# ScalarE fetches two function tables at other places: the root's in a distance attention, the sigmoid's in a quantized gated layer

## The reference, cut to what matters

```python
p = softmax(where(mask, scores, -1e32)) * mask
cum, tot = cumsum(p), sum(p)
dist = sqrt(clip((tot - cum) * abs(i - j), 0))
effect = clip(exp(dist * -softplus(gammas) * exp(sigmoid(pdiff))), 1e-5, 1e5)
scores = softmax(where(mask, scores * effect, -1e32))      # row 0 set to 0
out = scores @ v
```

```python
def act_qdq(x):
    scale = maximum(max(abs(x)) / 32767, 1e-12)
    return clip(round(x / scale), -32768, 32767) * scale
x = act_qdq(x)
up, gate = act_qdq(x @ w_up.T), act_qdq(x @ w_gate.T)
sig = clip(round(sigmoid(gate) * 65536), 0, 65535) / 65536
out = act_qdq(act_qdq(gate * sig) * up) @ w_down.T
```

## Time and profile before

| | |
|---|---|
| median of 3 runs | 1441.05 us (1440.38 to 1443.08) |
| the profiled execution | 1447.14 us |
| its span | 1445.4 us |
| PE, PEld busy | 943.6 us (65%), 610.1 us (42%) |
| DVE busy | 1015.2 us (70%) |
| ACT busy | 627.9 us (43%) |
| POOL busy | 123.2 us (9%) |

### The profile page before, as it was taken

How to read it: one execution, slowest core, us unless ns; L and a number is a source line. 1 busy time by engine, 2 the same in 40 slices (tenths; PEclk the granted TensorE clock), 3 DMA queues, 4 the chain that set the end, 5 groups by cost and what they waited for, 6 DMA issues and landing times. The chain is left out here.

```text
span 1445.4 us, 18406 instructions
## 1 busy us (share of the span) xinstructions
PE 943.6 (65%) x6190; PEld 610.1 (42%) x6190; DVE 1015.2 (70%) x2541; ACT 627.9 (43%) x1329; POOL 123.2 (9%) x261
## 2 busy tenths in 40 slices
PE   4864757555884204455978636999778526967977
PEld 2532333333553103345945313666445223534644
DVE  4868989835554899874448574999578596957833
ACT  3646666622432404443126425655046302634632
POOL 0120000000000000000120120000011021120100
PEclk9975555557986557667989857999679757988968
DMA  5000000001334001112000000000000000000000
GB/s 190 2 1 0 1 1 1 1 1 44 91 90 150 1 0 61 47 44 59 1 1 2 1 1 0 1 1 1 0 1 1 1 0 1 2 1 1 2 1 15
DMA packets 25997, 29.51 MB, mean 20 GB/s; under 512 B 689, under 2 KB 22577, under 8 KB 24882
## 3 DMA queue, kind: packets, MB, share of 16 engines
q1 hardware_dynamic: 25906, 28.35, 6.2%
HBM read 18.91 MB, written 9.44 MB: 20 GB/s over the span
## 5 line engine op out<-in xcount | busy, mean ns | idle before, releaser
L1750 DVE TENSOR_TENSOR_SCAN l2a_hs<-l2a_decay,l2a_b_ps 128x512 f32<-128x512 f32 x64 | 78.0, 1221 | 14.3 <-ACT l2a_decay L1680 6.1
L1605 PEld LDWEIGHTS l2a_b_ps<-l2a_diag,l2a_uT 128*128 128x128 f32 x512 | 64.0, 191 | 39.3 <-issue 38.0
L1605 PE MATMUL l2a_b_ps<-l2a_diag,l2a_uT 128*128 128x128 f32 x512 | 69.9, 280 | 2.0 <-DVE l2a_hs L1750 1.7
L2170 PE MATMUL l1w_mem_ps<-l1w_rows,l1w_post 128*128 128x64 f32 x16 | 4.6, 381 | 96.9 <-DVE l1w_rows L2313 96.9
L1613 PE MATMUL l2a_acc_ps<-l2a_hc,pack 128*128 128x512 f32 x128 | 65.5, 595 | 1.0 <-DVE l2a_hc L1761 1.0
L2286 DVE MATCH_REPLACE8 l1w_minus<-l1w_low,l1w_minus 128x129 f32<-128x129 f32 (+39 forms) x264 | 64.9, 283 | 0.0
L2280 DVE MAX8 l1w_low<-l1w_minus 128x8 f32<-128x129 f32 (+37 forms) x332 | 60.1, 278 | 0.8 <-DVE l1w_minus L2266 0.5
L2198 ACT ACTIVATE l1w_score<-l1w_mix_ps 128x264 f32<-128x264 f32 (+7 forms) x29 | 12.0, 451 | 111.7 <-DVE l1w_rows L2313 92.5
L2160 PE MATMUL l1w_mix_ps<-l1w_rows,l1w_pre 128*128 128x264 f32 (+7 forms) x58 | 30.9, 707 | 45.4 <-DMA l1w_rows<-scores_dram 37.7
L1680 ACT ACTIVATE l2a_decay<-l2a_dt,pack 128x1016 f32<-128x1016 f32 x32 | 36.4, 1141 | 45.4 <-DVE l2a_hs L1750 45.4
L917 ACT ACTIVATE l0x_prob<-l0x_dist,l0x_last_mx 128x128 f32<-128x128 f32 x128 | 38.3, 387 | 21.5 <-DVE l0x_last_mx L1039 21.5
(11 more groups left out here) (586 smaller groups left out, 2720.1 us busy)
## 6 DMA issues: line engine op xcount, KB each, us to landing
scores_dram<-l1p_dots SPq DMA_DIRECT2D x8, 1056.0 KB, 6.8
l1w_rows<-scores_dram SPq DMA_DIRECT2D x8, 1056.0 KB, 5.1
pack<-in_pack SPq DMA_DIRECT2D x1, 697.5 KB, 9.5
pack<-in_pack SPq DMA_DIRECT2D x2, 321.5 KB, 6.6
pack<-in_pack SPq DMA_DIRECT2D x1, 612.0 KB, 11.5
pack<-in_pack SPq DMA_DIRECT2D x1, 576.0 KB, 10.4
pack<-in_pack SPq DMA_DIRECT2D x1, 514.0 KB, 8.0
x_tok<-in_x SPq DMA_DIRECT2D x1, 512.0 KB, 4.2
```

The source lines that it names most:

```text
L1605: mm = nc.tensor.matmul(bx_ps(n)[:, j * S:(j + 1) * S], uT[:, c, b, :], diag[:, s % 2, b, :], start=True, stop=True)
L1750: nc.vector.tensor_tensor_scan(hs[:, n % 2, :], decay[:, k % 2, batches, :].rearrange("p b t -> p (b t)"), bx_ps(n), 0.0, ALU.mult, ALU.ad ...
```

## The change

In l0x a new one-column root, written to a tile that nobody reads, stands behind `copy_v`. The compiler therefore puts the root's table load in front of it, which is now ahead of three of the four `copy_probT`. In l2f a one-column sigmoid stands behind the copies of the transposed weights, and the three sigmoids stand ahead of up's six copies. Both new instructions raise a semaphore that nobody waits for.

```diff
+                def load_root_table():
+                    nc.scalar.activation(one_root[:], w("bq"), ACT.Sqrt, scale=0.0).then_inc(table_set, 1)
...
                     if inside(now):
                         first_weights(now, 1)
                         copy_v(now)
+                        load_root_table()
                     if inside(now - 1):
                         copy_probT(now - 1, 0, 1)
...
+                nc.scalar.activation(one_sig[:], cm.eps[:, 0:1], ACT.Sigmoid).then_inc(table_set, 1)
                 for h in range(2):
                     for c in range(CH2):
                         act.wait_ge(gate_read, CH2 * h + c + 1)
                         nc.scalar.activation(gate[:, c, cols(h)], ...)
+                for c in range(CH2):
+                    act.wait_ge(gate_q, c + 1)
+                    nc.scalar.activation(sig[:, c, :], gate[:, c, :], ACT.Sigmoid).then_inc(sig_set, 1)
                 for h in range(2):
                     for c in range(CH2):
                         act.wait_ge(up_read, CH2 * h + c + 1)
                         nc.scalar.activation(up[:, c, cols(h)], ...)
-                for c in range(CH2):
-                    act.wait_ge(gate_q, c + 1)
-                    nc.scalar.activation(sig[:, c, :], gate[:, c, :], ACT.Sigmoid).then_inc(sig_set, 1)
```

More of the change, by code:

```diff
@@ L771, in distance_attention @@
         o, oT = sc.sb("o", [128, D]), sc.sb("oT", [128, D])
+        one_root = sc.sb("one_root", [128, 1])
+        table_set = sc.sem("table_set")
         ln = LayerNorm(sc)
@@ L1304, in gated_ffn @@
         gate_step, last_inv = sc.sb("gate_step", [128, 1]), sc.sb("last_inv", [128, 1])
+        one_sig, table_set = sc.sb("one_sig", [128, 1]), sc.sem("table_set")
         norm = GroupNorm(sc)
```

## The result

| | before | after |
|---|---|---|
| median of 6 runs each, us | 1441.17 (1439.19 to 1445.38) | 1430.87 (1426.41 to 1434.52) |
| ratio, 95% interval | | 0.9925 [0.9903, 0.9947] |
| profiled execution: time, span, us | 1447.14, 1445.4 | 1434.52, 1432.7 |
| mean granted clock of TensorE in it | 0.764 | 0.769 |

The forecast was 1437.0 us, with a range of 1434.8 to 1440.0. The sign was right; 10.3 us were gained where 4.0 were worked out, and the result lies outside the range.

The account below looks back on a forecast made before the run. ScalarE's list, with its table loads, was taken to lie on the path VectorE waits for. Gains of 1.22 us in l0x and 2.81 in l2f, 4.0 together, off the median 1441.05 gave 1437.0 us, range 1434.8 to 1440.0.

Parts of the forecast that it names:

- The loads and the root: In l0x, moving the root's 1.30 us load ahead of the copies gains 0.24 us per steady step, 1.22 us together.
- d: In l0x, the delay of the copies caused by the moved load and small root: 0.83 us, bounds 0.73 and 0.95.
- the sums' copy: In l0x, ScalarE's copy behind the root: starts 1.80 us behind the last copy's start, at 211.33 against 211.57.
- the steady step: Steps 2 to 7 of l0x: 23.96 us instead of 24.20, 0.24 us won in each.
- (1): Rival: l0x gives nothing because the one-column root costs 0.37 us; 1438.2 us, chance 15%.
- (3): Rival: slower, a 1.38 us drain behind the load delays l0x's copies; 1446.7 us, chance 5% with others.
- (4): Rival: further gain, small root overlaps fully, 1.9 us in l0x; 1436.3 us, 68% together with the forecast.
- VectorE's wait for the effect: In l0x, VectorE's largest gap, 1.29 us, was to shrink to near 1.05.
- the wait before the division: In l0x, VectorE's 0.31 us wait for the sums was to shrink, the sums coming 0.24 us earlier.
- The sigmoids: In l2f, sigmoids ahead of up's copies remove VectorE's wait for the first sigmoid: gain 2.81 us.
- all behind it: Everything behind l2f's L1381, GpSimd included, was to move earlier by the same 2.81 us.
- Rival (2): l2f's gain half taken back, by copies and maxima slowing each other or another TensorE clock later; 1438.4 us, chance 12%.

Follow-up runs that it names:

- e3: The whole change again, timed against the kernel before: median 1444.66 us against 1447.12, ratio 0.9979.
- e2: Only the sigmoid's part in l2f, l0x as before, against the kernel before: median 1443.10 us against 1447.12, ratio 0.9966.
- e6: The whole change a third time, on another chip, against the kernel before: median 1434.87 us against 1446.55, ratio 0.9926.
- e7: Only the sigmoid's part in l2f again, on another chip, against the kernel before: median 1441.32 us against 1446.55, ratio 0.9970.
- e1: Only the root's part in l0x, l2f as before, against the kernel before: median 1447.37 us against 1447.12, ratio 1.0007.
- e8: The whole change plus two idle one-column VectorE copies late in l2f, against the kernel before: 1442.38 us against 1446.21, ratio 0.9964.
- e14: The whole change once more, in a later set, against the kernel before: median 1435.26 us against 1443.72, ratio 0.9957.
- e5: The change with load and small root moved behind the second of four copies (2.31 us idle), against the kernel before: 1430.93 us against 1446.55, ratio 0.9905.
- e10: Load in the 2.31 us gap, sigmoid's part, and two idle VectorE copies in l2f, against the kernel before: 1431.64 us against 1446.21, ratio 0.9892.
- e15: Repeat of the load in the 2.31 us gap with the sigmoid's part, against the kernel before: median 1432.50 us against 1443.72, ratio 0.9923.
- e4: The kernel before timed against itself, nothing changed: median 1446.62 us against 1447.12, ratio 0.9997.
- e11: The whole change plus fifteen idle one-column VectorE copies late in l2f, against the kernel before: 1446.85 us against 1446.21, ratio 1.0001.

## Why the prediction was wrong

**The loads and the root: right.** The load costs 1283 ns before and after. The Trainium skill, "ScalarE: Activation LUTs", section "What ACT_TABLE_LOAD costs", adds a drain of about 1380 ns; the trace has 0.02 us from the load's end to the small root. d was 0.84 (0.83 forecast), the sums' copy 1.80 us behind the last copy as forecast, the steady step 23.97 us (23.96). l0x gained 1.12 us of 1.22. Rivals (1) and (3), which stand on a larger d, are refuted, and so is (4), which needs d = 0.73.

**One reading of a wait was off, without effect.** I expected VectorE's wait for the effect to shrink to 1.05 us, and the wait before the division to shrink as well; the same 0.24 us cannot be taken from both. Both ends of the first wait moved together (1.28 us after), and the 0.31 us before the division vanished instead.

**The sigmoids: right.** 2.92 us against 2.81; no new wait behind, and GpSimd 0.93 us behind up's last copy, with 1 forecast.

**What failed is the step from places to program.** The prediction let "all behind it" move "by the same" and took 4.0 us off the median because "the two places have nothing to do with what differs between executions". Both halves of that are wrong:

- l0x's 1.1 us need not reach the end. e3 has lost all but 0.16 of its lead over e2 by the first matmuls of layer one, is 0.3 to 0.4 us behind e2 from 462 us to the end, and ends at a median 1.6 us above e2's. The profile after keeps 0.13 of 0.95 us at 460 us. Of e6's lead over e7, 0.7 of 1.0 us is still there at the end. e1's ratio of 1.0007 fits a loss, but does not show it.
- l2f's 2.9 us bring more than themselves, and not the same each time. e2 and e7 are 4.0 and 5.2 us below before by the medians. The whole change is 10.3, 2.5, 11.7 and 8.5 us below it in four measurements. What varies is how often the higher clock comes: with l2f's gain, at most slightly given back (e2, e3, e6, e7, e8, e14 and the first measurement), in 26 of 72 executions; with the load in the gap besides (e5, e10, e15) in 13 of 18; in the kernel before in 6 of 122, counting e4; in e1 and e11 in 0 of 24. Counted from a clock of 0.768 it is 30 of 72, 15 of 18, 12 of 122 and 0 of 24, so the order does not hang on where the line is drawn.

Rival (2) named "another clock of TensorE" in the later layers, but only as a loss of 1.4 us; with its sign open and the size of the 6.8 us measured it is what happened. The trace of before could have warned me: the profiled execution lay 6.1 us above the median, which I noted and set aside. Over 47 executions of the kernel before (with e4), the time falls by 0.98 us per 0.001 of mean clock (r² = 0.64): about two thirds of the spread between executions goes with it.

**What is open.** That l2f's half makes the higher clock more frequent is plain in the second and the last set (8 of 18 against 1 of 17; 7 of 12 against 3 of 53) and weak in the two others (3 of 24 against 1 of 59; 2 of 12 in e8, with a pause, against 3 of 53). What decides the single execution is not: e3 and e14 are one program on one chip, with 1 of 12 and 7 of 12. The position at which l3a is reached does not suffice.

**A better version.** The load in the larger gap is at 0.9905, 0.9923 and, with a small pause, 0.9892 of before; beside the change in the same sets it is 3.9 us (e5, e6), 2.8 us (e15, e14) and, both with the pause, 10.7 us (e10, e8) better by the medians, where 4.9 were won in l0x. It is clearly faster than the kernel before. Against the change all three differences have one sign, but the intervals of e5 and e6, and of e15 and e14, overlap.

## What to carry to other kernels

Put a table load into an idle stretch of ScalarE that is longer than load and small activation together, and look one place on for such a stretch before settling for a shorter one: 1.48 us fitted into 2.31, not into 0.58. Where TensorE's clock changes level within the kernel, local microseconds are not additive: price what lies behind by rows at both levels, keep that uncertainty with both signs in the range, and time on more than one occasion.

## What the runs showed of the hardware that I had not expected

- **Two courses of the clock in one program.** TensorE is busy about 81.3 or 75.2 us in the same stretch of l3x in most profiles (once 79.7, in e10); l3x and the end together differ by 8.4 us between e3 and e14. In the first measurement 6 of 6 executions had the higher clock and the change gained 10.3 us; in e3 it was 1 of 12 and 2.5 us.
- **A rise of the clock that stays where it was when the work moves.** In e2 and e3 it lies between 319 and 320 us, though the matmuls before it had started 1.37 us earlier in e3; the 16 of them took 10.04 us instead of 9.20.
- **A load does not wait for what its activation waits for.** In the first step of the kernel before the load goes at once, 6 us ahead of its root, which waits for VectorE. The row, from ScalarE's timeline of before:

```profile
108.08 1.28 ACT L906 ACT_TABLE_LOAD   x1
```
